# First attention of a four-layer network: scores in four quarter tiles of the array, keys and values projected apart, two small additions moved to GpSimd

## The chip, the cores and the metric

The kernel runs on one core of one Trainium2 chip. The metric is the time of one execution on the device, in microseconds (us). TensorE's instructions stand in the trace as PE (matmul) and PEld (weight load), VectorE's as DVE, ScalarE's as ACT, GpSimd's as POOL.

## The reference

Sixteen sequences of 256 tokens and 128 features pass four layers of attention and feed-forward blocks, with a modulation of the normalised input. The change touches the first attention alone. It has 64 query heads of width 64, eight key/value heads, a window of 128 keys, and one "sink" logit for each head:

```python
scores = jnp.einsum('bhqd,bhkd->bhqk', q, k) * scale
allowed = (qi >= kj) & (qi - kj < WINDOW)
scores = jnp.where(allowed[None, None], scores, neg)
logits = jnp.concatenate([scores, sink], axis=-1)
probs = jax.nn.softmax(logits, axis=-1)[..., :-1]
o = jnp.einsum('bhqk,bhkd->bhqd', probs, v)
return o.transpose(0, 2, 1, 3).reshape(B, S, H * HD) @ Wo.T + bo
```

All of it is in 32-bit floats.

## The kernel before

The first attention is cut into groups: one group is one sequence and one key/value head with its eight query heads, so there are 16 x 8 = 128 groups. A group has two units of four heads, 256 units in all. Each engine walks the same list of rounds (`attention_rounds`), one for each group n, and in a round works on three groups at once: scores and softmax of group n, the turning (transposition) of the weights of group n-1 (`turning`), values and output projection of group n-2 (`leaving`). The order of the instructions on each engine is written out by hand, and semaphores that count (`half`, `merged`, `masked`, `shift`, `exps`, `inv`, `norm`, `turn`, `side`, `free`) tie the engines together.

TensorE's order in a round is: scores of unit 2n (L484); values of both units of group n-2 (L520); scores of unit 2n+1; turning of unit 2n-2 (L176); projection q0 for the next group (L465); output projection of group n-2 (L507); in even rounds the projection "kv" of keys (L458) and values (L460) for groups n+2 and n+3; turning of unit 2n-1; projection q1 (L465). All projections write one PSUM bank, `a.side`, and each waits (`free`) until the one before it has been read out of that bank: q0 by ScalarE (L693), q1 (L573) and kv (L579 for keys, L582 for values) by VectorE.

A 32-bit matmul of the program is two pairs of weight load and matmul in the trace, so the counts there are twice those of the code. The scores of a unit are eight matmuls of the program: for each row half p of the array (partitions 64p to 64p+63 hold one head's 64 features), query tile qt and head j, 128 queries as weights against 128 keys (qt = 0) or 256 keys (qt = 1). The two row halves hold different weights and write different banks (`a.Sb[0]`, `a.Sb[1]`, and for qt = 0 the shared `a.Sb[2]`, the second user of which waits for `early`). Masked-off blocks are computed too.

VectorE's order in a round is: q1 out of the side bank; `masks` of unit 2n (two merges, L591, that fold the 256 keys into a window of 128, and eight mask-and-maximum operations, L603); `shift` (L623 the exponent's shift, L627 the sink's logit); `inverse` of unit 2n-1 (L633 adds the sink's weight to the sum, L636 the reciprocal); masks of 2n+1; `parted` of the turned weights (L613); shift; in even rounds kv out of the side bank; parted; inverse of unit 2n. ScalarE does the exponentials (L700), the sinks' (L724), and copies (L707, L713). GpSimd multiplies the weights by the reciprocals (L774), and every other round copies keys to the other row half (L764, L766).

At the end of each sequence, that is every eighth round, VectorE also takes out the sequence's result (L669), adds it to X (L677) and computes its statistics (L185, L187).

Of the kernel before, what the change touches and what calls it, by code (L numbers as in the profile page):

```python
# [12 lines left out]
ALU = mybir.AluOpType  # L13
ACT = mybir.ActivationFunctionType
AX = mybir.AxisListType.X
P = 128
# [373 lines left out]
def attention_plan(k, l, no, w, t_w):  # L390
    a = K()
    a.l, a.w, a.t_w, a.no = l, w, t_w, no
    a.nG, a.HG, a.d, a.CH = 8, 8, 64, 4
    a.scale = a.d ** -0.5
    a.groups, a.units = NB * a.nG, 2 * NB * a.nG
    R, G, W = Region(k.T, TW), Region(k.gbbc, 2048), Region(k.W3, width(SM))
    a.qT, a.kT = R.many(2, 1024), R.many(2, 512)
    a.nv = 3
    a.va = G.many(a.nv, 256)
    a.bk = R.get(a.nG // 2)  # L400
    a.Sm = R.many(2, 1024)
# [12 lines left out]

    a.uses = {}
    for part, n in [("q0", 0), ("kv", 0), ("q1", 0)] + [u for n in range(a.groups) for u in attention_ahead(a, n)]:
        a.uses[part, n] = len(a.uses)
    u = a.units
    a.s = sems(k, "a", zero=2, part=4, keys=a.groups // 2, early=u, half=3 * u, merged=2 * u, masked=3 * u, shift=u, sshift=u, exps=u, sexp=u, inv=u, norm=2 * u, turn=2 * u,
               even=u, odd=2 * u, values=u, o=u, side=len(a.uses), free=len(a.uses), out=a.groups, y=NB, yread=NB, x=NB)  # L420
    return a


# [3 lines left out]
def attention_ahead(a, n):  # L427


    out = [("q0", n + 1)] if n + 1 < a.groups else []  # L430
    out += [("kv", n + 2)] if n % 2 == 0 and n + 2 < a.groups else []
    return out + ([("q1", n + 1)] if n + 1 < a.groups else [])


def attention_rounds(a):


    for n in range(a.groups + 2):
        group = lambda lag: n - lag if 0 <= n - lag < a.groups else None
        ahead = n + 1 if n + 1 < a.groups else None  # L440
        kv = n + 2 if n % 2 == 0 and n + 2 < a.groups else None
        yield group(0), group(1), group(2), ahead, kv


def attention_pe(k, a, e):
# [6 lines left out]
    def project(step, n):  # L452
        b, g = divmod(n, a.nG)
        x = k.HT[:, b * 256:(b + 1) * 256]
        past(e, s["free"], a.uses[step, n])
        if step == "kv":

            e.matmul(a.side[:, 0:256], w["wk"][:, 128 * g + 64:128 * g + 192], x, start=True, stop=True)  # L458
            for j in range(2):
                done(e.matmul(a.side[:, 256 + 128 * j:384 + 128 * j], x[:, 128 * j:128 * j + 128],  # L460
                              w["wv"][:, 64 * g:64 * g + 128], start=True, stop=True), s["side"], j == 1)
        else:
            j = int(step[1])
            for c in range(2):
                done(e.matmul(a.side[:, 256 * c:256 * c + 256],  # L465
                              w["wq"][:, 512 * g + 128 * (2 * j + c):512 * g + 128 * (2 * j + c) + 128], x,
                              start=True, stop=True), s["side"], c == 1)

    def scores(i):


        n, s4 = divmod(i, 2)
        q, kt = a.qT[n % 2], a.kT[n // 2 % 2]
        e.wait_ge(*s["free"](taken(f"q{s4}", n)))
        e.wait_ge(*s["keys"](n // 2 + 1))
        past(e, s["masked"], 3 * i)
        for p, qt, j, last in ((0, 0, 0, 0), (1, 1, 0, 0), (0, 0, 1, 0), (0, 1, 0, 0), (1, 1, 1, 1), (0, 1, 1, 1),
                               (1, 0, 0, 0), (1, 0, 1, 1)):
            r, c, w_ = slice(64 * p, 64 * p + 64), 2 * s4 + j, 256 if qt else 128
# [43 lines left out]
    for step in ("q0", "kv", "q1"):  # L523
        project(step, 0)
    for n, turning, leaving, ahead, kv in attention_rounds(a):
        if n is not None:
            scores(2 * n)
        if leaving is not None:
            values(2 * leaving)
            values(2 * leaving + 1)  # L530
        if n is not None:
            scores(2 * n + 1)
        if turning is not None:
            turn(2 * turning)
        if ahead is not None:
            project("q0", ahead)
        if leaving is not None:
            out(leaving)
        if kv is not None:
            project("kv", kv)  # L540
        if turning is not None:
            turn(2 * turning + 1)
        if ahead is not None:
            project("q1", ahead)
        if leaving is not None and leaving % a.nG == a.nG - 1:
            e.wait_ge(*s["y"](leaving // a.nG + 1))
            for j in range(2):
                done(transpose(k, e, a.acc[:, 128 * j:128 * j + 128], a.yT[:, 128 * j:128 * j + 128]), s["yread"], j == 1)


def attention_dve(k, a, e):
# [15 lines left out]
    def project(step, n):  # L567
        g = n % a.nG
        e.wait_ge(*s["side"](a.uses[step, n] + 1))
        past(e, s["half"], 6 * (n - 1) if step == "q1" else 6 * (n - 2))  # L570
        if step == "q1":
            for c in range(2):
                done(e.tensor_scalar(a.qT[n % 2][:, 512 + 256 * c:768 + 256 * c], a.side[:, 256 * c:256 * c + 256],  # L573
                                     w["bq"][:, 4 * g + 2 + c:4 * g + 3 + c], None, ALU.add), s["free"], c == 1)
        else:

            m = n // 2
            kt = a.kT[m % 2]
            c_.then(e.tensor_scalar(kt[:, 0:256], a.side[:, 0:256], a.bk[:, g // 2:g // 2 + 1], None, ALU.add))  # L579
            past(e, s["values"], 4 * (m + 1 - a.nv))  # L580
            bv = w["bv"][:, 64 * g:64 * g + 128].unsqueeze(1).broadcast_to([P, 2, 128])
            e.tensor_tensor(a.va[m % a.nv].rearrange("p (t w) -> p t w", t=2),  # L582
                            a.side[:, 256:512].rearrange("p (t w) -> p t w", t=2), bv, ALU.add).then_inc(s["free"].sem, 1)

    old = k.C["mwin"][:, 0:128].unsqueeze(1).broadcast_to([P, 2, 128])

# [28 lines left out]
                              bank.rearrange("p (h w) -> p h w", h=4)).then_inc(s["odd"].sem, 1)  # L615

    def shift(i):
        ng, tk = a.ngs[i % 4], a.tks[i % 4]
        q0 = 8 * (i // 2 % a.nG) + 4 * (i % 2)
        over = lambda ap: ap[:, q0:q0 + 4].unsqueeze(1).broadcast_to([P, 2, 4])  # L620
        e.wait_ge(*s["masked"](3 * i + 3))
        past(e, s["exps"], i - 3)
        e.scalar_tensor_tensor(out=both(ng), in0=both(a.mxs[i % 4]), scalar=-a.scale, in1=over(a.nsink), op0=ALU.mult,  # L623
                               op1=ALU.min).then_inc(s["shift"].sem, 1)
        e.wait_ge(*s["shift"](i + 1))
        past(e, s["sexp"], i - 3)
        e.tensor_tensor(both(tk), both(ng), over(w["sink"]), ALU.add).then_inc(s["sshift"].sem, 1)  # L627

    def inverse(d):
        den, rin = a.dens[d % 4], a.rins[d % 4]  # L630
# [13 lines left out]
        mask(i, 0)  # L644
        mask(i, 2)

    project("kv", 0)
    for n, turning, leaving, ahead, kv in attention_rounds(a):
        if n is not None:
            project("q1", n)  # L650
# [8 lines left out]
        if n is not None:  # L659
            shift(2 * n + 1)  # L660
        if kv is not None:
            project("kv", kv)
# [90 lines left out]
def attention_pool(k, a, e):  # L753
# [5 lines left out]

    def both(n):  # L760
        kt = a.kT[n // 2 % 2]
        e.wait_ge(*s["free"](a.uses["kv", n] + 1))
# [4 lines left out]
        e.wait_ge(*s["keys"](n // 2 + 1))  # L767

    both(0)
# [2489 lines left out]
```

## Time and profile before

| | us |
|---|---|
| median of 3 runs | 4055.65 |
| lowest and highest of them | 4042.1, 4072.58 |
| profiled execution | 4066.91 |
| its span, first to last instruction | 4065.1 |

The span is 1.8 us shorter than the time of its execution; the profiled execution lies 11.3 us above the median. The first attention takes some 1526 us of the span (36 to 1562 us).

### The profile page before, as it was taken

Reading aid. Unit: us, or ns where it says so; the run is one execution under the profiler, and the core shown is the slowest. Engines: PE = TensorE matmul, PEld = TensorE weight load, DVE = VectorE, ACT = ScalarE, POOL = GpSimd, SP = SyncE. Lnnn points to the kernel's source line nnn. Section 1 sums busy time; section 2 is a strip of 40 time slices with the busy share of each in tenths; the row PEclk is TensorE's granted clock in tenths of the full one; section 3 lists DMA queues with packets and bytes.
Section 4 is the critical chain, followed back from the end, with each engine's and each line's share of the span. In section 5 each row is a group of like instructions: output and inputs, shape, how many; then the busy total and the mean of one; then the engine's idle time right before and its main releaser. Section 6 shows DMA issues by size and latency. Waiting matters only on the chain.

```text
span 4065.1 us, 77996 instructions
## 1 busy us (share of the span) xinstructions
PE 3728.0 (92%) x24958; PEld 2526.0 (62%) x24958; DVE 3141.8 (77%) x11783; ACT 2273.4 (56%) x6991; POOL 1346.0 (33%) x1227
## 2 busy tenths in 40 slices
PE   7999999999999999999998996998986999899865
PEld 5787877878778776666664443334555666555543
DVE  6888888888888886666777995776886778788771
ACT  5888888888878885225765443433333222377611
POOL 2333333343333331013544884551000000222116
PEclk9999999999999998986999998998997999899958
DMA  2000000000000001321000000000000000000023
GB/s 123 2 2 2 2 2 2 2 2 2 2 2 2 2 2 38 91 69 63 2 2 1 1 0 11 1 1 0 1 1 32 1 1 1 1 33 2 16 61 49
DMA packets 30836, 63.57 MB, mean 16 GB/s; under 512 B 3424, under 2 KB 19808, under 8 KB 29152
## 3 DMA queue, kind: packets, MB, share of 16 engines
q1 hardware_dynamic: 24288, 52.29, 3.7%
q0 software_dynamic: 6144, 6.30, 0.9%
q8 instruction: 204, 3.34, 0.3%
q14 instruction: 200, 1.64, 0.1%
HBM read 49.93 MB, written 8.65 MB: 14 GB/s over the span
## 4 chain that ended last, share of the span: by engine, by line
PE 68%; DVE 19%; issue 5%; ACT 5%; POOL 2%; DMA 1%; DVEq 0%; POOLq 0%; ACTq 0%; SPq 0%
PE ps L484 9%; PE ps L176 8%; PE ps L520 8%; PE ps L465 6%; PE ps L507 5%; PE ps L1621 3%; PE ps L1592 3%; PE ps L1590 3%; DVE gbbc L2284 2%; PE ps L2245 2%; PE ps L2232 2%; PE ps L961 2%; DVE gbbc L2273 2%; DVE gbbc L2279 2%; PE ps L939 2%
## 5 line engine op out<-in xcount | busy, mean ns | idle before, releaser
L603 DVE CUSTOM_DVE_ANT_0 T<-ps,C 128x128 f32<-128x128 f32 x2048 | 450.9, 285 | 0.0
L700 ACT ACTIVATE T<-T 128x128 f32<-128x128 f32 x1024 | 397.4, 391 | 42.9 <-DVE T L623 42.9
L484 PE MATMUL ps<-T 64*128 64x256 f32 (+1 forms) x4096 | 407.8, 339 | 11.3 <-DVE T L603 11.3
L484 PEld LDWEIGHTS ps<-T 64*128 64x128 f32 x4096 | 347.3, 188 | 113.1 <-issue 101.3
L774 POOL TENSOR_TENSOR T<-T 128x512 f32<-128x512 f32 x256 | 261.1, 1041 | 472.7 <-DVE T L636 472.7
L700 ACT ACTIVATE W<-T 128x128 f32<-128x128 f32 x1024 | 397.7, 392 | 27.8 <-DVE T L623 27.8
L774 POOL TENSOR_TENSOR W<-W,T 128x512 f32<-128x512 f32 x256 | 261.1, 1041 | 458.5 <-DVE T L636 458.5
L520 PE MATMUL ps<-W,gbbc 128*64 128x256 f32 x3072 | 359.8, 383 | 0.0
L613 DVE COPY_PREDICATED W<-gbbc,ps 128x512 f32<-128x512 int32 x512 | 341.9, 721 | 20.4 <-PE ps L176 20.4
L591 DVE COPY_PREDICATED ps<-C,ps 128x256 f32<-128x256 int32 x512 | 205.5, 429 | 143.6 <-PE ps L484 130.5
L176 PE MATMUL ps<-C,T 128*128 128x128 f32 (+1 forms) x1620 | 263.2, 300 | 50.8 <-DVE T L307 18.8
L1188 POOL TENSOR_TENSOR QK<-T,QK 128x512 fp32r<-128x512 f32 x128 | 162.1, 1276 | 383.4 <-ACT T L1148 258.0
L465 PE MATMUL ps<-HT,W 128*128 128x256 f32 x1024 | 272.6, 389 | 5.2 <-DVE gbbc L582 1.9
L520 PEld LDWEIGHTS ps<-W,gbbc 128*64 128x64 f32 x3072 | 209.0, 137 | 108.2 <-issue 0.3
L1127 ACT ACTIVATE T<-ps 128x384 f32<-128x384 f32 (+1 forms) x512 | 236.2, 550 | 71.3 <-PE ps L912 71.2
L176 PEld LDWEIGHTS ps<-C,T 128*128 128x128 f32 (+1 forms) x1620 | 195.8, 148 | 112.8 <-issue 23.0
L507 PE MATMUL ps<-T,W 128*128 128x256 f32 x1024 | 242.1, 379 | 0.8 <-ACT T L713 0.8
L1642 ACT ACTIVATE T<-ps,W 128x512 f32<-128x512 f32 x128 | 87.9, 687 | 240.4 <-PE ps L1590 240.3
L713 ACT ACTIVATE T<-ps 128x512 f32<-128x512 f32 x256 | 150.2, 587 | 127.5 <-PE ps L520 127.5
L507 PEld LDWEIGHTS ps<-T,W 128*128 128x128 f32 x1024 | 194.3, 190 | 27.6 <-issue 1.2
L176 PE MATMUL ps<-C,W 128*128 128x128 f32 x1202 | 168.5, 282 | 33.8 <-DMA W<-hrow_dram,T 14.3
L465 PEld LDWEIGHTS ps<-HT,W 128*128 128x128 f32 x1024 | 175.8, 192 | 34.4 <-DVE gbbc L582 19.2
(417 smaller groups left out, 8709.2 us busy)
## 6 DMA issues: line engine op xcount, KB each, us to landing
T<-crow_dram SPq DMA_DIRECT2D x128, 128.0 KB, 3.0
W<-in_l1f_dram SPq DMA_DIRECT2D x1, 6152.0 KB, 18.8
W<-in_l0a_dram SPq DMA_DIRECT2D x1, 5172.5 KB, 25.5
W<-in_l2f_dram SPq DMA_DIRECT2D x1, 3160.0 KB, 10.4
W<-in_l3f_dram SPq DMA_DIRECT2D x1, 3076.0 KB, 10.0
W<-in_sm_dram SPq DMA_DIRECT2D x1, 2729.0 KB, 9.7
W<-in_l0f_dram SPq DMA_DIRECT2D x1, 2256.0 KB, 29.9
X<-in_x_dram SPq DMA_DIRECT2D x1, 2048.0 KB, 8.1
```

The source lines that it names most:

```text
L176: return e.transpose(out, in_, k.C["ident"])
L465: done(e.matmul(a.side[:, 256 * c:256 * c + 256], w["wq"][:, 512 * g + 128 * (2 * j + c):512 * g + 128 * (2 * j + c) + 128], x, start=True ...
L484: m = e.matmul(o, q[r, 256 * c + 128 * qt:256 * c + 128 * qt + 128], kt[r, k0:k0 + w_], start=True, stop=True)
L507: done(e.matmul(a.acc[:, 0:256], w["wo"][:, (g * a.CH + c) * 128:(g * a.CH + c + 1) * 128], a.oT[n % 2][:, 256 * c:256 * c + 256], start=( ...
L520: done(e.matmul(bank[64 * r:64 * r + 64, at:at + 256], v[:, 128 * tile + g0:128 * tile + g0 + 64], x[:, r], start=(c != 1), stop=(c != 0)) ...
L591: e.copy_predicated(tiles[:, 0], old.bitcast(I32), tiles[:, 1]).then_inc(s["merged"].sem, 1)
L603: done(e.tensor_tensor_reduce(sm[:, at:at + 128], src, m, 1.0, -3.0e38, ALU.add, ALU.max, mx[:, col:col + 1]), s["masked"], x == (3 if ban ...
L613: e.copy_predicated(a.PT[t % 2][:, 512 * j:512 * j + 512].rearrange("p (h w) -> p h w", h=4), is_.unsqueeze(1).broadcast_to([P, 4, 128]).b ...
L700: done(e.activation(a.Pr[i % 4][:, at:at + w_], a.Sm[i % 2][:, at:at + w_], ACT.Exp, bias=a.ngs[i % 4][:, c:c + 1], scale=a.scale, accum_o ...
L774: e.tensor_tensor(pr, pr, a.rins[i % 4][:, c:c + 4].unsqueeze(2).broadcast_to([P, 4, 128]), ALU.mult).then_inc(s["norm"].sem, 1)
L1127: e.activation(a.PT[n % 2][:, 512 * g:512 * g + 256 + a.w1], a.far[g][:, 0:256 + a.w1], ACT.Exp, bias=0.0, scale=a.scale).then_inc(s["exp" ...
L1188: e.tensor_tensor(dst, a.whole[m % 2], dst.bitcast(F32), ALU.subtract).then_inc(s["low"].sem, 1)
```

## The change

Scores: each matmul of the program is cut by its 128 queries into two, of 64 queries each, which write partitions 0 to 63 and 64 to 127 of the same bank. The weights are thus 64 by 64 tiles, four places in the array (row half p, column half x). Each half skips 64 keys that the mask takes away for all its queries: with qt = 1 both halves stream 192 keys instead of 256, with qt = 0 the first 64 and the second 128. The order of the eight is changed. Bank 2 is set to zero once, since a part of it is now never written.

Keys and values: the step "kv" of even rounds becomes "k" in even rounds and "v" in odd rounds, each with its own turn in the side bank.

Small additions: L627 (sink's logit) and L633 (sum plus sink's weight) leave VectorE and are done by GpSimd, in the loop that multiplies by the reciprocals; a new semaphore count `summed` tells VectorE that the sum is there.

```diff
@@ attention_plan, attention_ahead
-    for part, n in [("q0", 0), ("kv", 0), ("q1", 0)] + ...
+    for part, n in [("q0", 0), ("k", 0), ("v", 0), ("q1", 0)] + ...
+def attention_side(a, n):
+    step, of = ("v", n + 1) if n % 2 else ("k", n + 2)
+    return (step, of) if of < a.groups else None
@@ attention_pe, scores
-        for p, qt, j, last in ((0, 0, 0, 0), (1, 1, 0, 0), (0, 0, 1, 0), (0, 1, 0, 0), (1, 1, 1, 1), (0, 1, 1, 1),
-                               (1, 0, 0, 0), (1, 0, 1, 1)):
+        for p, qt, j, last in ((0, 0, 0, 0), (1, 1, 0, 0), (0, 0, 1, 0), (1, 1, 1, 1), (0, 1, 0, 0), (1, 0, 0, 0),
+                               (0, 1, 1, 1), (1, 0, 1, 1)):
             if (p, qt, j) == (1, 0, 0):
                 e.wait_ge(*s["early"](i + 1))
             k0 = 256 * (n % 2 ^ p)
-            m = e.matmul(o, q[r, 256 * c + 128 * qt:256 * c + 128 * qt + 128], kt[r, k0:k0 + w_], start=True, stop=True)
-            done(m, s["half"], last)
-            done(m, s["early"], (p, qt, j) == (0, 0, 1))
+            for x in range(2):
+                k1, k2 = (64 * x, 192 + 64 * x) if qt else (0, 64 + 64 * x)
+                m = e.matmul(o[64 * x:64 * x + 64, k1:k2], q[r, 256 * c + 128 * qt + 64 * x:256 * c + 128 * qt + 64 * x + 64],
+                             kt[r, k0 + k1:k0 + k2], start=True, stop=True)
+                done(m, s["half"], last and x == 1)
+                done(m, s["early"], (p, qt, j, x) == (0, 0, 1, 1))
@@ attention_dve
-        e.wait_ge(*s["shift"](i + 1))
-        past(e, s["sexp"], i - 3)
-        e.tensor_tensor(both(tk), both(ng), over(w["sink"]), ALU.add).then_inc(s["sshift"].sem, 1)
...
-        e.wait_ge(*s["exps"](d + 1))
-        e.wait_ge(*s["sexp"](d + 1))
-        c_.then(e.tensor_tensor(den, den, a.ess[d % 4], ALU.add))
-        c_.hold(e)
+        e.wait_ge(*s["summed"](d + 1))
...
+    e.memset(a.Sb[2][:, :], 0.0).then_inc(s["part"].sem, 1)
@@ attention_pool
+    def sinks(i):
+        ...
+        e.wait_ge(*s["shift"](i + 1))
+        past(e, s["sexp"], i - 3)
+        e.tensor_tensor(tk..., ng..., sink..., ALU.add).then_inc(s["sshift"].sem, 1)
     both(0)
+    sinks(0)
     for i in range(a.units):
+        if i + 1 < a.units:
+            sinks(i + 1)
+        den = a.dens[i % 4]
+        e.wait_ge(*s["exps"](i + 1))
+        e.wait_ge(*s["sexp"](i + 1))
+        e.tensor_tensor(den, den, a.ess[i % 4], ALU.add).then_inc(s["summed"].sem, 1)
         e.wait_ge(*s["inv"](i + 1))
```

## Rows read from the trace of the kernel before

**Rows 1.** The page, parts 1 and 4: busy time, and the chain that ended last.

```profile
PE 3728.0 (92%) x24958; PEld 2526.0 (62%) x24958; DVE 3141.8 (77%) x11783; ACT 2273.4 (56%) x6991; POOL 1346.0 (33%) x1227
...
PE ps L484 9%; PE ps L176 8%; PE ps L520 8%; PE ps L465 6%; PE ps L507 5%; PE ps L1621 3%; PE ps L1592 3%; PE ps L1590 3%; DVE gbbc L2284 2%; PE ps L2245 2%; PE ps L2232 2%; PE ps L961 2%; DVE gbbc L2273 2%; DVE gbbc L2279 2%; PE ps L939 2%
```

**Rows 2.** Windows view, eight rounds: length, busy (count) by engine, PE clock, DMA.

```profile
625.78:720.08 94.30, 93.75 (x734) 75.35 (x732) 79.49 (x415) 76.35 (x321) 35.80 (x41) 1.00 0.01 2
```

**Rows 3.** Timeline of PE in an odd round: start us, length us, line, operation.

```profile
600.83 1.58 PE L484 MATMUL ps<-T 64*128 64x128 f32 x16
602.34 2.81 PE L520 MATMUL ps<-W,gbbc 128*64 128x256 f32 x24
605.08 1.58 PE L484 MATMUL ps<-T 64*128 64x128 f32 x16
...
608.38 1.89 PE L507 MATMUL ps<-T,W 128*128 128x256 f32 x8
610.11 1.04 PE L176 MATMUL ps<-C,T 128*128 128x128 f32 x8
```

**Rows 4.** Timeline of PE in the even round that follows.

```profile
611.94 1.58 PE L484 MATMUL ps<-T 64*128 64x128 f32 x16
...
618.63 1.03 PE L465 MATMUL ps<-HT,W 128*128 128x256 f32 x4
619.49 1.89 PE L507 MATMUL ps<-T,W 128*128 128x256 f32 x8
621.22 0.59 PE L458 MATMUL ps<-HT,W 128*128 128x256 f32 x2
621.65 0.61 PE L460 MATMUL ps<-W,HT 128*128 128x128 f32 x4
622.10 1.04 PE L176 MATMUL ps<-C,W 128*128 128x128 f32 x8
623.17 1.13 PE L465 MATMUL ps<-HT,W 128*128 128x256 f32 x4
624.23 1.58 PE L484 MATMUL ps<-T 64*128 64x128 f32 x16
```

**Rows 5.** Groups by line and shape, weight loads: busy us, mean ns, idle before.

```profile
L484 PEld LDWEIGHTS ps<-T 64*128 64x128 f32 x4096 | 347.3, 188 | 113.1 <-issue 101.3
L520 PEld LDWEIGHTS ps<-W,gbbc 128*64 128x64 f32 x3072 | 209.0, 137 | 108.2 <-issue 0.3
```

**Rows 6.** Timeline of PE in later layers, four column tiles of 32 columns.

```profile
3702.16 1.07 PE L939 MATMUL ps<-T 128*32 128x256 f32 x16
...
2482.76 5.32 PE L2209 MATMUL ps<-W,T 128*32 128x128 f32 x128 [0.78 <-DVE T L2311]
```

**Rows 7.** Timeline of DVE in that even round.

```profile
613.24 0.81 DVE L591 COPY_PREDICATED ps<-C,ps 128x256 f32<-128x256 int32 x2
...
615.76 0.17 DVE L623 SCALAR_TENSOR_TENSOR T<-T 128x8 f32<-128x8 f32 x1
...
616.24 0.20 DVE L636 RECIPROCAL T<-T 128x8 f32<-128x8 f32 x1
617.48 0.81 DVE L591 COPY_PREDICATED ps<-C,ps 128x256 f32<-128x256 int32 x2 [1.04 <-PE ps L484]
...
622.70 0.41 DVE L582 TENSOR_TENSOR gbbc<-ps,W 128x256 f32<-128x256 f32 x1
```

**Rows 8.** Waits view, 100 to 1500 us: total us, times, longest us.

```profile
PEld ps L465 <- DVE gbbc L582: 16.3, 60, 0.3
```

**Rows 9.** Timeline of POOL in the two rounds.

```profile
603.94 0.40 POOL L766 COPY T<-T 64x256 f32<-64x256 f32 x1
605.47 2.04 POOL L774 TENSOR_TENSOR T<-T 128x512 f32<-128x512 f32 x2 [1.13 <-DVE T L636]
```

**Rows 10.** Timelines at a sequence's end: DVE, and PE's wait after it.

```profile
633.71 0.54 DVE L669 TENSOR_SCALAR gbbc<-ps,W,modT 128x256 f32<-128x256 f32 x1
...
640.30 1.58 PE L484 MATMUL ps<-T 64*128 64x128 f32 x16 [0.42 <-DVE T L603]
```

More of the change, by code:

```diff
@@ L415, in attention_plan @@
     a.uses = {}
-    for part, n in [("q0", 0), ("kv", 0), ("q1", 0)] + [u for n in range(a.groups) for u in attention_ahead(a, n)]:
+    for part, n in [("q0", 0), ("k", 0), ("v", 0), ("q1", 0)] + [u for n in range(a.groups) for u in attention_ahead(a, n)]:
         a.uses[part, n] = len(a.uses)
     u = a.units
-    a.s = sems(k, "a", zero=2, part=4, keys=a.groups // 2, early=u, half=3 * u, merged=2 * u, masked=3 * u, shift=u, sshift=u, exps=u, sexp=u, inv=u, norm=2 * u, turn=2 * u,
+    a.s = sems(k, "a", zero=2, part=5, keys=a.groups // 2, early=u, half=3 * u, merged=2 * u, masked=3 * u, shift=u, sshift=u, exps=u, sexp=u, inv=u, norm=2 * u, turn=2 * u,
                even=u, odd=2 * u, values=u, o=u, side=len(a.uses), free=len(a.uses), out=a.groups, y=NB, yread=NB, x=NB)
+    a.s |= again(k, "soft", summed=("gather", u))
     return a
@@ L430, in attention_ahead @@
     out = [("q0", n + 1)] if n + 1 < a.groups else []
-    out += [("kv", n + 2)] if n % 2 == 0 and n + 2 < a.groups else []
+    out += [attention_side(a, n)] if attention_side(a, n) else []
     return out + ([("q1", n + 1)] if n + 1 < a.groups else [])
+def attention_side(a, n):
+    step, of = ("v", n + 1) if n % 2 else ("k", n + 2)
+    return (step, of) if of < a.groups else None
 def attention_rounds(a):
@@ L440, in attention_rounds @@
         ahead = n + 1 if n + 1 < a.groups else None
-        kv = n + 2 if n % 2 == 0 and n + 2 < a.groups else None
-        yield group(0), group(1), group(2), ahead, kv
+        yield group(0), group(1), group(2), ahead, attention_side(a, n)
 def attention_pe(k, a, e):
@@ L455, in project @@
         past(e, s["free"], a.uses[step, n])
-        if step == "kv":
-            e.matmul(a.side[:, 0:256], w["wk"][:, 128 * g + 64:128 * g + 192], x, start=True, stop=True)
+        if step == "k":
+            e.matmul(a.side[:, 0:256], w["wk"][:, 128 * g + 64:128 * g + 192], x, start=True,
+                     stop=True).then_inc(s["side"].sem, 1)
+        elif step == "v":
             for j in range(2):
-                done(e.matmul(a.side[:, 256 + 128 * j:384 + 128 * j], x[:, 128 * j:128 * j + 128],
+                done(e.matmul(a.side[:, 128 * j:128 * j + 128], x[:, 128 * j:128 * j + 128],
                               w["wv"][:, 64 * g:64 * g + 128], start=True, stop=True), s["side"], j == 1)
@@ L476, in scores @@
         past(e, s["masked"], 3 * i)
-        for p, qt, j, last in ((0, 0, 0, 0), (1, 1, 0, 0), (0, 0, 1, 0), (0, 1, 0, 0), (1, 1, 1, 1), (0, 1, 1, 1),
-                               (1, 0, 0, 0), (1, 0, 1, 1)):
-            r, c, w_ = slice(64 * p, 64 * p + 64), 2 * s4 + j, 256 if qt else 128
+        for p, qt, j, last in ((0, 0, 0, 0), (1, 1, 0, 0), (0, 0, 1, 0), (1, 1, 1, 1), (0, 1, 0, 0), (1, 0, 0, 0),
+                               (0, 1, 1, 1), (1, 0, 1, 1)):
+            r, c = slice(64 * p, 64 * p + 64), 2 * s4 + j
             o = a.Sb[p][:, 256 * j:256 * j + 256] if qt else a.Sb[2][:, 256 * p + 128 * j:256 * p + 128 * j + 128]
@@ L521, in values @@
                               start=(c != 1), stop=(c != 0)), s["values"], c == 2 and r == 1)
-    for step in ("q0", "kv", "q1"):
+    for step in ("q0", "k", "v", "q1"):
         project(step, 0)
+    e.wait_ge(*s["part"](5))
     for n, turning, leaving, ahead, kv in attention_rounds(a):
@@ L539, in attention_pe @@
         if kv is not None:
-            project("kv", kv)
+            project(*kv)
         if turning is not None:
@@ L569, in project @@
         e.wait_ge(*s["side"](a.uses[step, n] + 1))
-        past(e, s["half"], 6 * (n - 1) if step == "q1" else 6 * (n - 2))
+        if step != "v":
+            past(e, s["half"], 6 * (n - 1) if step == "q1" else 6 * (n - 2))
         if step == "q1":
@@ L574, in project @@
                                      w["bq"][:, 4 * g + 2 + c:4 * g + 3 + c], None, ALU.add), s["free"], c == 1)
+        elif step == "k":
+            kt = a.kT[n // 2 % 2]
+            e.tensor_scalar(kt[:, 0:256], a.side[:, 0:256], a.bk[:, g // 2:g // 2 + 1], None,
+                            ALU.add).then_inc(s["free"].sem, 1)
         else:
             m = n // 2
-            kt = a.kT[m % 2]
-            c_.then(e.tensor_scalar(kt[:, 0:256], a.side[:, 0:256], a.bk[:, g // 2:g // 2 + 1], None, ALU.add))
             past(e, s["values"], 4 * (m + 1 - a.nv))
@@ L582, in project @@
             e.tensor_tensor(a.va[m % a.nv].rearrange("p (t w) -> p t w", t=2),
-                            a.side[:, 256:512].rearrange("p (t w) -> p t w", t=2), bv, ALU.add).then_inc(s["free"].sem, 1)
+                            a.side[:, 0:256].rearrange("p (t w) -> p t w", t=2), bv, ALU.add).then_inc(s["free"].sem, 1)
     old = k.C["mwin"][:, 0:128].unsqueeze(1).broadcast_to([P, 2, 128])
@@ L617, in shift @@
     def shift(i):
-        ng, tk = a.ngs[i % 4], a.tks[i % 4]
+        ng = a.ngs[i % 4]
         q0 = 8 * (i // 2 % a.nG) + 4 * (i % 2)
@@ L645, in masks @@
         mask(i, 2)
-    project("kv", 0)
+    e.memset(a.Sb[2][:, :], 0.0).then_inc(s["part"].sem, 1)
+    project("k", 0)
+    project("v", 0)
     for n, turning, leaving, ahead, kv in attention_rounds(a):
@@ L661, in attention_dve @@
         if kv is not None:
-            project("kv", kv)
+            project(*kv)
         last = leaving is not None and leaving % a.nG == a.nG - 1
@@ L761, in both @@
         kt = a.kT[n // 2 % 2]
-        e.wait_ge(*s["free"](a.uses["kv", n] + 1))
+        e.wait_ge(*s["free"](a.uses["k", n] + 1))
         past(e, s["norm"], 4 * n - 6)
@@ L767, in both @@
         e.wait_ge(*s["keys"](n // 2 + 1))
+    def sinks(i):
+        ng, tk = a.ngs[i % 4], a.tks[i % 4]
+        q0 = 8 * (i // 2 % a.nG) + 4 * (i % 2)
+        e.wait_ge(*s["shift"](i + 1))
+        past(e, s["sexp"], i - 3)
+        e.tensor_tensor(tk.rearrange("p (t h) -> p t h", t=2), ng.rearrange("p (t h) -> p t h", t=2),
+                        a.w["sink"][:, q0:q0 + 4].unsqueeze(1).broadcast_to([P, 2, 4]), ALU.add).then_inc(s["sshift"].sem, 1)
     both(0)
+    sinks(0)
     for i in range(a.units):
+        if i + 1 < a.units:
[4 more added lines that the diff above has]
+        e.tensor_tensor(den, den, a.ess[i % 4], ALU.add).then_inc(s["summed"].sem, 1)
         e.wait_ge(*s["inv"](i + 1))
```

## The prediction, made before the changed kernel ran

> **What bounds the kernel now.** I read the page first. PE is busy 92% of the span, and scores (L484), turning (L176), values (L520), projections (L465) and output (L507) lead the chain that ended last [rows 1]. A share over the whole span mixes layers, so next come eight rounds of the attention: 94.30 us, of which PE is busy 93.75, DVE 79.49, ACT 76.35, POOL 35.80, at a granted clock of 1.00, the 2.4 GHz level [rows 2]. Then the timeline of PE. In the odd round each piece starts where the one before ends: 1.51 us from scores to values, 2.74 for values, 1.73 for eight matmuls of the output projection; scores come again 11.11 us after the last [rows 3, 4]. So what PE saves in a round, the round saves, as long as no other engine gets in its way. An even round takes 12.29 us (611.94 to 624.23), 1.18 more [rows 4].
>
> **Scores.** First the price of a matmul. Eight matmuls of 256 columns take 1.73 us, 0.216 each; four of 128 take 0.45 (621.65 to 622.10 [rows 4]), and half of 0.216 is 0.108; I take 0.109. So the price goes by the column, and I estimate 192 at 0.162 and 64 at 0.055. From start to end one of 128 is 0.28 long (eight turning matmuls span 1.04, less seven spacings [rows 4]). A unit's scores on one row half are 4 instructions of 128 and 4 of 256: 4 x 0.109 + 4 x 0.216 = 1.30 us. Both halves do the same, and the whole call takes 1.51, so the halves overlap fully already; the other 0.21 is the first weight load and the emptying before the next piece [rows 3].
>
> After the change there are four places. The busiest (x = 1) has 4 instructions of 128 and 4 of 192: 4 x 0.109 + 4 x 0.162 = 1.08 us; x = 0 has 4 x 0.055 + 4 x 0.162 = 0.87. If the four run at once, the call is 1.08 + 0.21, less 0.05 because the first load has 64 columns (137 against 188 ns, [rows 5]): 1.24, a gain of 0.27. I give 0.05 back, for the second user of bank 2: its place is free some 0.70 us into the call, and that is just when `early` can arrive (the fourth instruction of 128 starts at 0.38 and is 0.28 long, plus some 0.05 to be seen), so its weight load is exposed. That leaves 1.28, a gain of 0.23 a call, 256 x 0.23 = 59 us; without the give-back 69.
>
> Do four places run at once? The trace has no 64 by 64 tile. The nearest rows are column tiles of 32: 16 matmuls of 128x256 in 1.07 us, which one after the other would take 16 x 0.216 = 3.45 and two at a time 1.73; so four are in flight [rows 6]. They share the weights' side differently than two rows by two columns would, but rows two at a time (scores) and columns two at a time (values: 24 of 0.216 in 2.74 us, half of 5.18) are both there [rows 3]. A second question is whether PE takes 64 instructions (32 loads, 32 matmuls) in 1.08 us, 34 ns a pair. The 128 pairs of L2209 took 5.32 us, 42 ns a pair, with smaller loads and part of it at a lower clock [rows 6]; that is the bound from above: 32 x 0.042 = 1.33, a call of 1.49, a gain of 0.02.
>
> The Trainium skill ("TensorE: Matmul & The Clock Gate", Part 3, The mechanism) says that matmuls are strictly first in, first out in start and end, and that a weight load overlaps a running matmul only when its row group differs. The 16 matmuls of L939 speak against both: in program order each tile's two instructions stand together and all tiles share the row group, yet four are in flight [rows 6]. What the page's order would do here is the first rival.
>
> **Keys and values apart.** The extra 1.18 us of an even round are kv's matmuls, 0.88 (621.22 to 622.10), and 0.30 of waiting: q1 starts at 623.17 with its load exposed, where eight turning matmuls from 622.10, at 0.109 each, are past at 622.97 [rows 4]. It waits for the values' additions L582, started at 622.70 [rows 7], 60 times in the waits view [rows 8]. Apart, the matmuls cost the same, 0.43 for k and 0.44 for v, in different rounds. Each is read out by one operation (0.4 to 0.5 us) that can start some 0.65 us after its first matmul; it is done about 1.17 us after, and q1's load is due at 0.43 + 0.87 - 0.11 = 1.19. So the wait goes with 0.02 to spare: 64 x 0.30 = 19 us. What is late next is q1 itself, by no more than those hundredths. k and v each must wait until ScalarE has read q0, as kv did: q0's matmuls start at 618.63, its readers are done near 620.5, and the side bank is wanted at 621.22 [rows 4].
>
> **VectorE and GpSimd.** VectorE loses L627 and L633, some 0.3 us a unit, all of it beside PE's work: nothing directly. But `inverse` of unit 2n-1 follows the shift of unit 2n at once, and now waits for GpSimd, which first does the next unit's sink addition (free to start when the shift is done) and then the sum. Queued behind that wait are the merges of unit 2n+1, and behind those PE. Times from the start of scores(2n): the shift ends at 3.83 now (615.76 + 0.17 - 611.94 = 3.99, less 0.15 since the merges can start earlier); PE will have the half scores of 2n+1 ready for the merge at about 5.05 (now 617.48 - 611.94 = 5.54, less 0.23 and 0.26 for two shorter calls). Two GpSimd additions of d each and two semaphores fit if 3.88 + 2d + 0.2 is under 5.05, so d under 0.48. The trace has no 8-column addition on GpSimd. Bounds: not below nothing; above, 1.04 for a 128x512 multiplication (2.04 for two); nearest in size is a copy of 64x256 at 0.40 [rows 9]. I take 0.2 to 0.4: hidden in VectorE's idle 1.04 [rows 7]. GpSimd has 4.5 of 11.8 us of work a round, so its own queue takes it; the key copies and multiplications behind the new additions have rounds to spare.
>
> **Other chains.** From the end of the output projection, VectorE's path to the next scores(2n+1) (parted, reciprocal, q1, merges, masks) comes to 5.85 us by the same rows, PE's to 0.44 + 0.87 + 0.96 + 1.28 + 2.74 = 6.29: 0.4 to spare. Not so at a sequence's end: there VectorE has L669, L677 and the statistics too, and PE already waits 0.42 us [rows 10]. The v addition is now in that round: it comes before L669 and moves all that follows by 0.34; VectorE saves 0.12 (L633) and 0.1 before it, and PE arrives 0.23 earlier. PE's wait grows to about 0.9, so 0.4 of the gains is given back in each of 15 sequences' ends: 6 us. At the start one more drain of the side bank: 1 us. The zeroing is a few tenths, once, and hidden behind the first projections.
>
> **Sum.** 59 + 19 - 6 - 1 = 71 us less. On the profiled execution's 4066.9 that is 3996; on the median of the runs, 11.3 below it, 4055.65 - 71 = 3985.
>
> **Rivals.**
> 1. *Two at a time.* If a place's second instruction holds up the next place's first, so that no more than two of the four run at once, a call takes the sum over the 16 halves: 8 x 0.162 + 4 x 0.109 + 4 x 0.055 = 1.95, plus 0.16: 2.11, that is 0.60 more than now. 256 x 0.60 = 154, less 13 for the other parts: +141, 4197. It decides as soon as a call takes longer than 1.51 us. For it: no row has both kinds of tile at once, and the order in the code puts the two instructions of a place together. Against it: L939. The skill's order (same section) would give this time. Chance 0.14.
> 2. *PE's intake or the weights bound the call* at 1.3 to 1.5: gain of 0.02 to 0.10, some 5 to 26 us, with the side bank's 13: 4017 to 4037. For it: 42 ns a pair in L2209. Against it: part of that ran at a lower clock. Chance 0.12.
> 3. *GpSimd is slow*: at d = 1.04 the merges of 2n+1 come 1.1 us late; 0.8 of it is room before PE's second turning call needs `parted`, 0.35 x 128 = 45 us are lost: 4030. Chance 0.06.
> 4. *The scores gain is there but k or v no longer fits* (q1 waits as before, now in both rounds): 20 to 40 us lost, 4005 to 4025. Chance 0.05.
>
> **How the numbers follow.** The main case has 0.63, and its own range is 3965 (no give-back, no growth at the ends: 69 + 19 + 3 = 91) to 4005. Cases 2 to 4 end by 4037, so 3963 to 4040 holds 0.85 of the chance; case 1 is left out. Faster by over 1% (below 4015): the main case and a part of 4 and 2, 0.68. Within 1%, about what a measurement of this kernel can tell from no change (its three runs lie 0.75% apart): the rest of 2 to 4, 0.18. Slower by over 1%: 0.14.
>
> **What will show it.** In the profile after: scores to values 1.24 to 1.28 us apart (2.11 if rival 1 holds, 1.4 to 1.5 for rival 2); even and odd rounds alike, near 11.0 us; the wait of L465 for the values' additions gone; eight rounds in some 89.9 us; idle of VectorE before the merges still put down to PE. Were it put down to GpSimd, rival 3 holds. A longer wait than 0.9 before the second scores at a sequence's end would show VectorE to be the next bound.

## The result, and the profile after

The changed kernel takes 3994.8 us (median of 4 runs, 3991.2 to 3996.2), the kernel before beside it 4054.6 (4 runs): ratio 0.985, 95% interval 0.981 to 0.989. The profiled execution took 3991.2 us, 75.7 less than that of the kernel before. Not all of this is the attention's: its last output projection ends at 1500.3 us after and at 1565.7 before (a little behind the 1562 given above), 65.3 less; what follows it, untouched by the change, took 2489.0 against 2499.5. A second profile of the changed kernel has 2494.8 there, and other profiles below 2484 to 2501, so 10 us between two profiles mean nothing. Nor does the start say much: the first output projection stands at 79.4 us in the first profile of the changed kernel and at 75.6 in the second, where the granted clock from 36 to 80 us was 0.65 and 0.81. In between, the full rounds of both kernels repeat to 0.02 us, but for one of the kernel before, and most of what follows reads them. A round is measured from one output projection to the next.

An odd round of TensorE (from 600.39), parts of the next one, which ends a sequence's work (the wait at 616.59), and the start of the one after, as in [rows 3, 4] before: start, length, line, operation. Scores are L494 now, values L531, output L518, q0 and q1 L473, keys L464, values' projection L468.

```profile
600.39 1.37 PE L494 MATMUL ps<-T 64*64 64x64 f32 x32
601.69 2.81 PE L531 MATMUL ps<-W,gbbc 128*64 128x256 f32 x24
604.43 1.37 PE L494 MATMUL ps<-T 64*64 64x64 f32 x32
605.73 1.09 PE L176 MATMUL ps<-C,T 128*128 128x128 f32 x8
...
609.25 0.61 PE L468 MATMUL ps<-W,HT 128*128 128x128 f32 x4
...
616.59 1.37 PE L494 MATMUL ps<-T 64*64 64x64 f32 x32 [0.74 <-DVE T L618]
...
621.41 0.59 PE L464 MATMUL ps<-HT,W 128*128 128x256 f32 x2
621.84 1.04 PE L176 MATMUL ps<-C,W 128*128 128x128 f32 x8
622.72 1.03 PE L473 MATMUL ps<-HT,W 128*128 128x256 f32 x4
623.67 1.37 PE L494 MATMUL ps<-T 64*64 64x64 f32 x32
```

A call of scores takes 1.30 us, 0.21 less than before (601.69 - 600.39, as 605.73 - 604.43). Behind the keys' projection the turning starts at 621.84 and q1 at 622.72, 0.88 later with no gap: before, 1.07 lay there. A round now takes 11.12 to 11.14 us, odd or even, where 12.29 and 11.11 took turns; the one at a sequence's end takes 12.16, before 11.82. There PE waits 0.74 us for the masks (L618), in place of 0.42 [rows 10].

Eight rounds in the windows view (length, PE, PEld, DVE, ACT, POOL, clock), the answer to [rows 2]:

```profile
614.47:704.51 90.04, 89.30 (x990) 70.48 (x988) 75.32 (x383) 75.49 (x320) 41.83 (x72) 1.00 0.01 2
```

From output projection to output projection, 94.33 us a sequence have become 90.05 (means of fifteen), at the same granted clock of 1.00: PE still bounds the rounds, busy for 89.30 of 90.04 us, and the rest is the one wait of 0.74. Of VectorE's 79.5 us 75.3 are left, GpSimd has 41.8 for 35.8.

VectorE and GpSimd around the new wait, timelines of the same round:

```profile
603.94 0.17 DVE L638 SCALAR_TENSOR_TENSOR T<-T 128x8 f32<-128x8 f32 x1
604.63 0.20 DVE L645 RECIPROCAL T<-T 128x8 f32<-128x8 f32 x1 [0.53 <-POOL T L796]
605.46 0.81 DVE L606 COPY_PREDICATED ps<-C,ps 128x256 f32<-128x256 int32 x2 [0.62 <-PE ps L494]
```

```profile
604.24 0.20 POOL L785 TENSOR_TENSOR T<-T,W 128x8 f32<-128x8 f32 x1 [0.53 <-POOL T L777]
604.40 0.20 POOL L796 TENSOR_TENSOR T<-T 128x8 f32<-128x8 f32 x1
```

The shift ends at 604.11, GpSimd's two additions of 0.20 follow, and VectorE stands idle for 0.53 us before its reciprocal; the merges behind it wait for PE all the same, another 0.62.

The first 0.03 us of the call of scores at 604.43, one line of the kernel alone (`--source L494`, window 604.40 to 604.46): count, shortest, median and longest in ns, first and last start, shapes.

```profile
L494 PEld LDWEIGHTS ps<-T x4: 129/129/129, 604.4 to 604.4; 64*64 64x64 f32 x4
L494 PE MATMUL ps<-T x4: 267/346/373, 604.4 to 604.5; 64*64 64x192 f32 x2, 64*64 64x64 f32 x1, 64*64 64x128 f32 x1
```

All four places have started: one with 64 columns, one with 128, two with 192. In this call the four matmuls start within 0.020 us.

### The profile page after: what moved, and what is told of

It is laid out like the page before. It is cut to its first block, busy times and chain, and to the rows that moved or that the text cites. A ratio compares the mean times of both kernels' runs of the same rounds, so it can differ in the third digit from the quotient of the medians.

```text
span 3989.3 us, 86187 instructions
## 1 busy us (share of the span) xinstructions
PE 3650.1 (91%) x29054; PEld 2445.8 (61%) x29054; DVE 3076.4 (77%) x11272; ACT 2259.0 (57%) x6991; POOL 1440.9 (36%) x1739
## 4 chain that ended last, share of the span: by engine, by line
PE 67%; DVE 18%; issue 6%; ACT 5%; POOL 2%; DMA 1%; DVEq 0%; POOLq 0%; ACTq 0%; SPq 0%
PE ps L494 8%; PE ps L176 8%; PE ps L531 8%; PE ps L518 6%; PE ps L473 5%; PE ps L1647 3%; PE ps L1618 3%; PE ps L1616 3%; PE ps L2258 2%; PE ps L2271 2%; DVE gbbc L2310 2%; PE ps L987 2%; DVE gbbc L2299 2%; DVE gbbc L2305 2%; PE ps L951 2%
## 5 line engine op out<-in xcount | busy, mean ns | idle before, releaser
L618 DVE CUSTOM_DVE_ANT_0 T<-ps,C 128x128 f32<-128x128 f32 x2048 | 450.8, 285 | 0.0
L494 PE MATMUL ps<-T 64*64 64x192 f32 (+2 forms) x8192 | 354.0, 296 | 15.8 <-DVE T L618 15.8
L531 PE MATMUL ps<-W,gbbc 128*64 128x256 f32 x3072 | 359.8, 383 | 0.0
L494 PEld LDWEIGHTS ps<-T 64*64 64x64 f32 x8192 | 271.2, 134 | 127.0 <-issue 106.2
L531 PEld LDWEIGHTS ps<-W,gbbc 128*64 128x64 f32 x3072 | 209.5, 137 | 114.1 <-issue 21.8
L473 PE MATMUL ps<-HT,W 128*128 128x256 f32 x1024 | 267.5, 384 | 2.2 <-ACT HT L334 1.1
L518 PE MATMUL ps<-T,W 128*128 128x256 f32 x1024 | 242.0, 379 | 0.8 <-ACT T L724 0.8
L785 POOL TENSOR_TENSOR T<-T,W 128x8 f32<-128x8 f32 x256 | 51.1, 200 | 456.4 <-DVE T L638 423.3
L518 PEld LDWEIGHTS ps<-T,W 128*128 128x128 f32 x1024 | 194.3, 190 | 27.6 <-issue 1.2
```

The costliest lines, as they stand in the source:

```text
L473: done(e.matmul(a.side[:, 256 * c:256 * c + 256], w["wq"][:, 512 * g + 128 * (2 * j + c):512 * g + 128 * (2 * j + c) + 128], x, start=True ...
L494: m = e.matmul(o[64 * x:64 * x + 64, k1:k2], q[r, 256 * c + 128 * qt + 64 * x:256 * c + 128 * qt + 64 * x + 64], kt[r, k0 + k1:k0 + k2], s ...
L518: done(e.matmul(a.acc[:, 0:256], w["wo"][:, (g * a.CH + c) * 128:(g * a.CH + c + 1) * 128], a.oT[n % 2][:, 256 * c:256 * c + 256], start=( ...
L618: done(e.tensor_tensor_reduce(sm[:, at:at + 128], src, m, 1.0, -3.0e38, ALU.add, ALU.max, mx[:, col:col + 1]), s["masked"], x == (3 if ban ...
```

## The experiments

Each run is the changed kernel with the edit shown. "By the rounds" means the mean length of a sequence, less the changed kernel's 90.05 us, times 16.

**The scores as before, the rest of the change kept.** The old order of the eight matmuls comes back with them.

```diff
-            for x in range(2):
-                k1, k2 = (64 * x, 192 + 64 * x) if qt else (0, 64 + 64 * x)
-                ...
-                m = e.matmul(o[64 * x:64 * x + 64, k1:k2], ...)
+            w_ = 256 if qt else 128
+            m = e.matmul(o, q[r, 256 * c + 128 * qt:256 * c + 128 * qt + 128], kt[r, k0:k0 + w_], start=True, stop=True)
```

> The changed kernel, with the scores as before: two row halves, 128 queries as weights, all 256 or 128 keys, the old order of the eight. Keys and values stay apart, the additions stay on GpSimd. My theory (PE bounds every round and the scores call gave 1.51 - 1.30 = 0.21 us): scores to values 1.51 us again, a regular round 11.13 + 0.42 = 11.55 us, time 3995 + 50 = 4045 (one call in sixteen lies in the wait at a sequence's end and counts for nothing). Rival (the rounds became shorter by the side bank and VectorE's relief, the scores' saving is hidden): below 4010.

Measured: 4042.8 us (10 runs), ratio to the kernel before 0.995 (0.992 to 0.997). Its timeline of PE has 1.51 us from scores to values again:

```profile
603.09 1.58 PE L493 MATMUL ps<-T 64*128 64x128 f32 x16
604.60 2.81 PE L529 MATMUL ps<-W,gbbc 128*64 128x256 f32 x24
607.34 1.58 PE L493 MATMUL ps<-T 64*128 64x128 f32 x16
```

Regular rounds take 11.55 us, a sequence 93.22, 3.17 more than in the changed kernel; times 16 that is 51 us, and the medians differ by 48. The rival is out: the scores carry some three quarters of the 4.28 us that a sequence became shorter. The new order by itself was not tried.

**Four places, but all keys.**

```diff
-                k1, k2 = (64 * x, 192 + 64 * x) if qt else (0, 64 + 64 * x)
+                k1, k2 = (0, 256) if qt else (0, 128)
```

> The changed kernel with the four places, but each streams all 256 or 128 keys, masked-off blocks too. My theory (each place needs 4 x 0.109 + 4 x 0.216 = 1.30 us as each half did before, so quartering by itself gives only the shorter weight load, and the gain is the keys left out; the wait for bank 2 is hidden too, since the second row half is busy for longer): call 1.44 to 1.46 us, time 3995 + 0.15 x 240 = 4031. Rival (four places raise the throughput by themselves): call 1.30 or less, 3995. Rival (PE's intake of 64 instructions sets the call): also 1.30, unchanged.

Measured: 4031.9 us (10 runs), ratio 0.994 (0.992 to 0.996).

```profile
608.99 1.53 PE L494 MATMUL ps<-T 64*64 64x128 f32 x32
610.45 2.38 PE L531 MATMUL ps<-W,gbbc 128*64 128x256 f32 x20
```

(The second row is cut off by the end of its view.) The call takes 1.46 us, rounds 11.45. Quartering the array by itself is worth 0.05 us of 1.51, about what the shorter first weight load saves; the other 0.16 of the gain are the keys left out. Both rivals, 1.30 or less, are out.

**Keys and values together again**, with the new scores and GpSimd's additions: the steps, waits and side bank of `kv` as before.

```diff
-    step, of = ("v", n + 1) if n % 2 else ("k", n + 2)
...
+        kv = n + 2 if n % 2 == 0 and n + 2 < a.groups else None
```

> The changed kernel with keys and values projected together in even rounds, as before. My theory: the wait of q1 for the values' addition comes back, 0.3 us in each of 64 even rounds, rounds alternate between about 10.7 and 11.9 us; at the ends of sequences the shorter odd round gives some 0.3 us back in 15 cases: 3995 + 19 - 5 = 4009. Rival (the split only moves matmuls between rounds): 3995.

Measured: 4003.2 us (4 runs), ratio 0.987 (0.981 to 0.992).

```profile
600.85 1.04 PE L176 MATMUL ps<-C,W 128*128 128x128 f32 x8
601.91 1.13 PE L466 MATMUL ps<-HT,W 128*128 128x256 f32 x4
602.98 1.37 PE L487 MATMUL ps<-T 64*64 64x64 f32 x32
```

Rounds take 10.69 and 11.86 us, together 0.30 more than the changed kernel's two. The turning starts at 600.85 and its eight are past 0.88 later at 601.73; q1 stands at 601.91 with the first load still to come (its row is 1.13 long instead of 1.03), and from the turning to the next scores it is 2.13 us instead of 1.83. The round at a sequence's end takes 11.61, and 91.12 a sequence are 1.07 more than 90.05, so 17 us; the medians differ by 8 to 10. The round times decide between the theories, the medians of two lots of four runs agree in sign only.

**The additions back on VectorE.**

```diff
+        e.tensor_tensor(both(tk), both(ng), over(w["sink"]), ALU.add).then_inc(s["sshift"].sem, 1)
...
+        e.wait_ge(*s["exps"](d + 1))
+        e.wait_ge(*s["sexp"](d + 1))
+        c_.then(e.tensor_tensor(den, den, a.ess[d % 4], ALU.add))
+        c_.hold(e)
-        e.wait_ge(*s["summed"](d + 1))
...
-            sinks(i + 1)                 # GpSimd's two additions go
```

> The changed kernel with the two small additions back on VectorE. My theory (VectorE has room in regular rounds and bounds only the ends of sequences): regular rounds stay at 11.13 us, the round at a sequence's end grows from 12.16 by 0.1 to 0.3: 3995 + 2 to 5, say 3998. Rival (VectorE's relief is worth its 0.3 us a unit): +20 to +70. Rival (the new wait of VectorE for GpSimd, 60 us in the waits view, costs): below 3990.

Measured: 3989.6 us (4 runs), ratio 0.982 (0.978 to 0.987). Regular rounds are unchanged to 0.01 us, the round at a sequence's end takes 12.37 instead of 12.16: 3 us in all, in the direction expected; the median of four runs lies 3 to 5 us the other way, within what such medians scatter. Taken by itself, 3989.6 would just meet the second rival's "below 3990", but that rival needs shorter rounds, and none is shorter. The first rival's 20 us or more are not there. So the move is worth 3 us by the rounds and nothing that a time can show.

The three parts of the change, taken back one at a time, cost 3.17, 1.07 and 0.21 us a sequence, 4.45 together; the whole change saved 4.28. They meet in the round at a sequence's end, so an exact sum was not to be expected, and little is left for a fourth cause.

**GpSimd made later, by 3, 10 and 6 additions.** The sink addition is repeated, each repetition waiting for the last.

```diff
+        for _ in range(3):    # 10, 6
+            c_.then(e.tensor_tensor(tk..., ng..., sink..., ALU.add))
+            c_.hold(e)
```

> The changed kernel with GpSimd's sink addition done four times instead of once, each waiting for the last (about 0.25 us each, so 0.75 us more before the sum). My theory (VectorE's reciprocal may come that late: the merges behind it wait for PE until 0.6 us after it, and what they feed has 0.9 us of room): rounds 11.13 us, time 3995. Rival (GpSimd's additions are already at the edge and bound the round): 0.75 us more in each of 128 rounds, 4090.

Measured: 3991.5 us, ratio 0.984 (0.979 to 0.988), rounds 11.12 to 11.14 and 12.16: no change at all.

> The same with eleven instead of one, some 2.6 us more before the sum. My theory: 2.6 less 0.6 less 0.9 of room, so about 1.1 us more in each of 128 rounds, 12.2 us a round and 4135. Rival (VectorE's wait for GpSimd is hidden at any length, since the chain's PE work covers it): 3995. If it costs much more than 1.1 a round, GpSimd itself (10 of 11 us busy) or ScalarE has become the bound.

Measured: 4346.1 us, ratio 1.072 (1.066 to 1.077), rounds 13.89 and 13.94. That is 2.8 us more a round, not 1.1. VectorE's timeline shows what I had left out:

```profile
604.36 0.20 DVE L645 RECIPROCAL T<-T 128x8 f32<-128x8 f32 x1 [1.69 <-POOL T L800]
...
611.14 0.20 DVE L645 RECIPROCAL T<-T 128x8 f32<-128x8 f32 x1 [3.28 <-POOL T L800]
```

It waits for GpSimd at both reciprocals of a round, 5.0 us together, and PE then waits for masks and for `parted`. Neither GpSimd nor ScalarE has become the bound by its own work: in the 120 us from 600 they were busy 78.3 and 79.1.

> The changed kernel with GpSimd's sink addition done seven times instead of once: six more at 0.28 us, 1.68 us later sums. My theory after the two doses before (two places where VectorE waits: behind the first shift of a round 0.63 us and then 0.9 us further on are free, behind the second 1.74 us): only the first is late, by 1.05 us, of which 0.9 is room: rounds 11.15 to 11.4 us, time 3997 to 4030. Rival (the lateness goes straight into the round): 1.05 a round, 4130.

Measured: 4063.3 us (10 runs), ratio 1.003 (1.001 to 1.004), rounds 11.66 to 11.71: 0.56 more a round, where I had expected 0.02 to 0.3 and the rival 1.05. Both fall. The rows of VectorE, then of PE:

```profile
605.29 0.20 DVE L645 RECIPROCAL T<-T 128x8 f32<-128x8 f32 x1 [2.21 <-POOL T L800]
605.41 0.75 DVE L606 COPY_PREDICATED ps<-C,ps 128x256 f32<-128x256 int32 x2
...
609.05 0.42 DVE L597 TENSOR_TENSOR gbbc<-ps,W 128x256 f32<-128x256 f32 x1
609.39 1.33 DVE L628 COPY_PREDICATED W<-gbbc,ps 128x512 f32<-128x512 int32 x2
611.29 0.20 DVE L645 RECIPROCAL T<-T 128x8 f32<-128x8 f32 x1 [0.57 <-POOL T L800]
```

```profile
603.03 1.37 PE L494 MATMUL ps<-T 64*64 64x64 f32 x32
...
608.29 0.60 PE L176 MATMUL ps<-C,T 128*128 128x128 f32 x4
609.23 0.63 PE L176 MATMUL ps<-C,T 128*128 128x128 f32 x4 [0.34 <-DVE W L628]
```

PE loses nearly all of its time in one place (0.50 of 0.58 in this round): the second half of the turning starts 0.94 us after the first instead of 0.44, because the merges of unit 2n+1 started 2.38 us into their scores call instead of 1.03, 1.35 late and not 1.05. Of this, 1.68 is GpSimd's doing (the reciprocal starts 2.20 behind the shift instead of 0.52) and 0.38 is that the shift itself ends later against PE, 0.06 behind the start of that scores call instead of 0.32 ahead; 0.71 are taken up ahead of the merges, where VectorE had stood idle for 0.62. The 0.38 goes with the second wait, 0.57 us, which I had called free. In the changed kernel VectorE waits 0.65 us there for PE's projection; once VectorE is late, that wait is gone (L597 follows at once) and its slack with it. Rooms found one by one don't add up. What stands between three and six repetitions was not tried.

**VectorE's work at a sequence's end moved.** The result of the sequence is read out of PSUM ahead of the keys or values; the addition to X goes behind the next round's first shift, the two statistics behind the next two second shifts.

```diff
+        added()                       # X += result, after shift(2n) of the next round
         if turning is not None:
             inverse(2 * turning + 1)
...
             shift(2 * n + 1)
-        if kv is not None:
-            project(*kv)
+        counted()                     # one bn_stats, bn_aggr
...
+        if kv is not None:            # after the read-out of the result
+            project(*kv)
         if turning is not None:
             parted(2 * turning + 1)
...
-            e.tensor_tensor(x, x, a.acc[:, 0:256], ALU.add).then_inc(s["x"].sem, 1)
-            ...                       # and the two stats
+            ended.append(b)
```

> The changed kernel with VectorE's work at the end of a sequence moved: the result's read-out before the values' read-out (into VectorE's wait for it), the addition to X behind the next round's first shift (into its wait for GpSimd), the two statistics one each behind the next two rounds' second shift (into the wait for keys or values). My theory (the 12.16 us round is VectorE's chain, and PE's own path there is 11.13 + 0.21): that round 11.34 us, 15 x 0.8 = 12 us less: 3983. Rival (the moved work delays the side bank or the merges instead): neighbouring rounds grow, total 3990 or more.

Measured: 3972.5 us (4 runs), ratio 0.979 (0.974 to 0.983). The end round takes 11.35 us, the others stay; 89.23 us a sequence, 13 less in all by the rounds, as expected. The median, 3983 by the expectation, is 19 us below that of the run with three more additions, whose rounds are the changed kernel's, and 22 below the changed kernel's; what the 6 to 9 us beyond the rounds are stays open. Part of the start goes with the granted clock: here the first output projection stands at 73.5 us, at a clock of 0.88 from 36 to 80 us. PE's second scores at a sequence's end follow values without a wait (616.88 - 614.13 = 2.75):

```profile
612.84 1.37 PE L494 MATMUL ps<-T 64*64 64x64 f32 x32
614.13 2.81 PE L531 MATMUL ps<-W,gbbc 128*64 128x256 f32 x24
616.88 1.36 PE L494 MATMUL ps<-T 64*64 64x64 f32 x32
```

**Only the first of these moves**, the result read out ahead of the values.

> The changed kernel with only the first of these moves: the sequence's result is read out before the values. My theory: VectorE's chain at a sequence's end loses the 0.34 us by which the values' read-out had pushed it: that round 11.82 us, time 3990. Rival (the growth of the end round from 11.82 to 12.16 had another cause): 12.16 stays.

Measured: 3989.8 us (4 runs), ratio 0.983 (0.978 to 0.988). The end round takes 12.04 us, not 11.82. VectorE then has:

```profile
609.24 0.41 DVE L597 TENSOR_TENSOR gbbc<-ps,W 128x256 f32<-128x256 f32 x1
609.65 1.35 DVE L628 COPY_PREDICATED W<-gbbc,ps 128x512 f32<-128x512 int32 x2
610.89 0.20 DVE L645 RECIPROCAL T<-T 128x8 f32<-128x8 f32 x1
611.18 0.42 DVE L688 TENSOR_TENSOR X<-X,ps 128x256 f32<-128x256 f32 x1
```

The addition to X starts 0.29 us behind the reciprocal, in the changed kernel 0.10: being earlier, it now waits for PE's two transposes of the result, which end at 611.14. And the read-out of the result itself waits 0.21 for the output projection. So 0.12 of the expected 0.34 came.

**The moved ends, and the additions back on VectorE.**

> VectorE's work at a sequence's end moved as in the run that did so (3972.5), and the two small additions back on VectorE as well. My theory (outside the ends VectorE has room for them, and the ends now have it too): rounds 11.13 and 11.35 us, time within 5 us of 3972. Rival (the additions on GpSimd are what makes the moved work fit): end rounds longer by 0.2 to 0.3, some 4 us more.

Measured: 3969.2 us (4 runs, 3967.7 to 3971.8), ratio 0.978 (0.976 to 0.980); rounds 11.12 to 11.14 and 11.35, 89.24 a sequence. This and the run with the ends alone moved are the fastest that compute everything, and can't be told apart; they beat both kernels.

**The changed kernel again.**

> The changed kernel as it is, on the chip of these runs, to stand beside them: rounds 11.13 and 12.16 us, time 3990 to 3997. What its part after the first attention takes beside 2489 us in its other profile shows how much of a difference between two profiles is not the attention's.

Measured: 3992.9 us (4 runs), ratio 0.984 (0.980 to 0.987); rounds to 0.01 us those of its first profile, and 2494.8 us behind the attention.

**No wait for bank 2.** The first half's 128-key scores go to bank 0, where its later ones overwrite them. So this kernel leaves those scores out of the softmax; its other work is all there.

```diff
-            if (p, qt, j) == (1, 0, 0):
-                e.wait_ge(*s["early"](i + 1))
+            if (p, qt) == (0, 0):
+                o = a.Sb[0][:, 256 * j:256 * j + 128]
```

> The changed kernel, with the first row half's 128-key scores written to bank 0 instead of bank 2 (where its later scores overwrite them), so that bank 2 has one writer and the wait for it goes. It leaves out those scores from the softmax; every instruction but the wait is there. My theory (the second half's places stand free until the wait for bank 2 is over, 0.07 us a call, the give-back of the prediction): call 1.23 us, rounds 11.0, time 3993 - 0.066 x 240 = 3977. Rival (the last 0.07 of a call is PE's intake of 64 instructions or the change of tile shape): call stays at 1.30, time 3993.

Measured: 3973.5 us (4 runs), ratio 0.980 (0.978 to 0.983). Rounds 11.02 and 11.04, at a sequence's end 12.12; 89.32 a sequence, 12 us less in all by the rounds. The median is 19 to 21 less; the 7 to 9 beyond the rounds are not explained, as above.

```profile
602.47 1.32 PE L494 MATMUL ps<-T 64*64 64x64 f32 x32
603.71 2.81 PE L531 MATMUL ps<-W,gbbc 128*64 128x256 f32 x24
```

The call takes 1.25 us: 0.05 of the 0.07 was the wait. That leaves 0.01 to the 1.24 worked out for a call without it, which is within the rounding of the prices.

## Why the prediction was right

The forecast was 3985, the median is 3995, inside the main case's own range. Term by term:

1. *PE bounds the rounds.* Shown: with the scores as before, each regular round grew by 0.42 us, twice the 0.21 of a call.
2. *Scores, 0.23 a call, 59 us.* The call measured 1.297, not 1.28: a gain of 0.21, 54 us. This term was 5 us too large. Four places run at once, and the call goes by its busiest one. The price by the column held: in the changed kernel's trace, matmuls of one place that follow each other start 0.162 apart with 192 columns, 0.109 with 128 and 0.058 with 64, where 0.162, 0.109 and 0.055 were taken. The calls fit too: 1.46 with all keys, where 4 x 0.109 + 4 x 0.216 + 0.16 gives the same, and 1.25 with 128 and 192 columns and no wait, where 1.08 + 0.16 gives 1.24. The give-back for bank 2 was put at 0.05, and 0.05 is what its removal brought. It came about as described: in the call at 604.43 the last of the four instructions that bank 2 waits for starts at 0.385 and is 0.269 long, the waiting load starts at 0.71, and the busiest place's next matmul follows 0.159 after the first instead of 0.109.
3. *Rivals 1 and 2.* Two at a time would have been 2.11, an intake of 42 ns a pair 1.49; the call took 1.30. An intake of one pair in some 40 ns is out by the rows as well: four loads and four matmuls start within 0.03 us. The four places are two in each row half, so loads and matmuls of one row half run together. So the trace speaks for a 64 by 64 tiling too against the Trainium skill ("TensorE: Matmul & The Clock Gate", Part 3, The mechanism), where it lets a load overlap a running matmul only when its row group differs. The strict order of starts, the other half of rival 1, fails as well if the two instructions of a place stand together in the order of issue, as the prediction took it: the other three places start first, and the second instruction of the first place 0.106 us in.
4. *Keys and values apart, 19 us.* 0.30 for two rounds, as said; with them together again the wait returned in the same place. The 0.02 to spare held: q1's wait of [rows 8] no longer stands in the waits view, and both kinds of round are alike to 0.02 us.
5. *GpSimd.* An addition took 0.20, the low end of what I took for d, and the wait of 0.53 lies in time that VectorE spent waiting for PE. The times worked out for this place were close: the shift ends 3.72 after the start of scores (3.83 in the prediction, and 3.88 in its next sentence, a slip without effect), and the merges start at 5.07 (5.05). Three repetitions more cost nothing. But the room was overstated: 0.56 us a round were lost at six repetitions, where rival 3's way of counting gives less than 0.3. That rival's price for d = 1.04, 45 us, is then likely too low for the same reason: it took one wait a round, there are two, and they share their slack. No run has a d of 1.04. (By its own numbers, 1.1 less 0.8, it was 0.3 a round and not 0.35.)
6. *The ends, 6 us back.* The end round exceeds the others by 1.03 instead of 0.71: 0.32 x 15 = 5 us. The chain is VectorE's, as said: moving its work brought the round to 11.35. What the prediction did not draw from this step is that these ends, 0.8 us x 15, were worth moving.
7. *The start, 1 us.* No run shows this term. The first output projection stands at 79.4 us in the changed kernel's first profile and at 77.8 before, but the granted clock from 36 to 80 us was 0.65 there and 0.81 before. At 0.81 too, the changed kernel's second profile has it at 75.6, earlier than before. What a read-out more costs is lost in this.
8. *Sum.* 54 + 19 - 5 = 68. By the rounds, 94.33 - 90.05 = 4.28 us in each of 16 sequences are 68 as well, and from the first output projection to the end of the last the time fell from 1487.9 to 1421.0, 66.9 less. The medians differ by 59.8; the 7 us between were not traced. They are no more than the part behind the attention scatters from profile to profile, and the kernel before spreads over 30 us. That the forecast of the median lies 10 off and not 3 is thus as much this scatter as the scores' term.

## What to carry to other kernels

When several places of TensorE's array work at once, cost a call by the columns that the busiest place streams: cutting the weights finer brought next to nothing by itself here (0.05 of 1.51 us); it brings the freedom to leave different columns out in each place, and that freedom is the gain. Where one engine is busy without a gap, take its savings at full price, but recompute for the rounds out of the ordinary (ends of sequences) which engine is behind: work of another engine that is free elsewhere is paid in full there, and can be moved into its waits in the next round. Slack before two waits of one engine in one loop is one slack, not two. Before a difference in the start of a program is put down to a change, compare the granted clock there.

## What the runs showed of the hardware

- Four 64 by 64 tiles (two row halves, two column halves) run fully at once: 32 weight loads and 32 matmuls of 64, 128 and 192 columns in 1.30 us, at a granted clock of 1.00, the 2.4 GHz level. The first matmuls of the four start within 0.020 us. In one place, matmuls that follow each other start 0.058, 0.109 and 0.162 us apart with 64, 128 and 192 columns.
- GpSimd does an addition of 128x8 in 0.20 us; two independent ones start 0.16 apart, ones that wait for each other 0.28 apart (ten in 2.72 us). A 128x8 addition on VectorE was 0.14 to 0.17 long, so GpSimd is hardly slower for so small a one; from the end of VectorE's shift (604.11) to the start of its reciprocal lay 0.52 us by way of GpSimd.
